# Four moves in a Perceiver block's hand-ordered loop: an earlier query load, an earlier self-attention context, split latent-sum copies, later setup steps

## The reference

```python
def attend(x, latents, mask, ...):            # x = ctx_1024, latents = layernorm(x)
    xn = layernorm(x, ln_x_g, ln_x_b)
    ln = layernorm(latents, ln_l_g, ln_l_b)
    q = ln @ Wq                                # 16 heads of 64
    kv = concatenate((xn, ln), axis=1) @ Wkv
    sim = einsum('bhid,bhjd->bhij', q, k)      # masked keys: -max
    out = einsum('bhij,bhjd->bhid', softmax(sim), v)
    return layernorm(out @ Wout, ln_o_g, ln_o_b)
x = x + attend(ctx_1024, _layernorm(x), mask, ...)
x = x + self_attention(_layernorm(x), Wq, ..., slopes)   # 64 rows, 16 heads of 8, ALiBi
x = x + feed_forward(_layernorm(x), ...)       # fake-quantised, scale from max|x| of all rows
```

## Time and profile before

| | |
|---|---|
| median of 3 runs | 866.89 us (865.94 to 867.53) |
| the profiled execution | 870.95 us |
| its span | 869.2 us |
| granted clock over the span | 0.956 |
| body 0, body 1 | 45.1, 54.3 us |
| a body of the loop (13 of them) | 47.07 us |
| PE, DVE, ACT, POOL busy in such a body | 45.6, 33.5, 34.6, 31.8 us |

### The profile page before, as it was taken

How to read it: one execution, slowest core, us unless ns; L and a number is a source line. 1 busy time by engine, 2 the same in 40 slices (tenths; PEclk the granted TensorE clock), 3 DMA queues, 4 the chain that set the end, 5 groups by cost and what they waited for, 6 DMA issues and landing times.

```text
span 869.2 us, 22523 instructions
## 1 busy us (share of the span) xinstructions
PE 780.4 (90%) x7063; PEld 423.7 (49%) x7063; DVE 605.6 (70%) x1515; ACT 587.0 (68%) x1017; POOL 521.7 (60%) x660
## 2 busy tenths in 40 slices
PE   5697899999999999999999999999999999997753
PEld 4343444545455455545454545545554545454412
DVE  5787566676777776666767677767666776756487
ACT  5387577776767676868777676767676877763242
POOL 3277356676757666666767675766666676764101
PEclk9799899999999999999999999999999999999655
DMA  6212212121221112121212122110212121200001
GB/s 191 56 42 81 71 43 68 43 62 52 57 56 52 49 26 63 41 72 38 71 41 61 52 57 56 54 48 26 62 41 72 39 71 40 67 17 16 4 0 49
DMA packets 98349, 45.86 MB, mean 53 GB/s; under 512 B 65956, under 2 KB 90376, under 8 KB 98184
## 3 DMA queue, kind: packets, MB, share of 16 engines
q1 hardware_dynamic: 98256, 45.37, 18.8%
q10 hardware_dynamic: 56, 0.05, 0.0%
HBM read 25.70 MB, written 3.27 MB: 33 GB/s over the span
## 4 chain that ended last, share of the span: by engine, by line
PE 65%; DVE 19%; ACT 7%; issue 7%; POOL 1%; DVEq 1%; DMA 1%; ACTq 1%; SPq 0%; POOLq 0%
PE bank L1399 14%; PE bank L1458 7%; DVE mx L1799 7%; PE bank L1362 7%; PE bank L1317 5%; PE bank L1366 5%; PE bank L1364 4%; PE bank L1475 3%; PE bank L1519 3%; PE bank L1334 3%; PE bank L1504 2%; PE bank L1494 2%; ACT arena L1080 2%; ACT arena L1065 2%; DVE xtT_l L1782 1%
## 5 line engine op out<-in xcount | busy, mean ns | idle before, releaser
L832 POOL TENSOR_TENSOR p<-arena,p 128x512 f16<-128x512 f32 x256 | 299.5, 1170 | 180.3 <-ACT arena L1065 179.5
L1062 ACT ACTIVATE p<-bank,maskbias 128x512 f16<-128x512 f32 x224 | 155.2, 693 | 138.2 <-PE bank L1366 137.6
L1799 DVE TENSOR_REDUCE mx<-bank 128x1 f32<-128x512 f32 x256 | 165.8, 685 | 37.9 <-PE bank L1334 36.6
L1399 PE MATMUL bank<-p,xv 128*128 128x512 f16 (+1 forms) x768 | 183.9, 382 | 5.2 <-ACT arena L1080 2.7
L1065 ACT ACTIVATE arena<-bank,maskbias 128x512 f32<-128x512 f32 x224 | 154.3, 689 | 0.0
L1399 PEld LDWEIGHTS bank<-p,xv 128*128 128x128 f16 (+1 forms) x768 | 58.0, 97 | 73.2 <-issue 23.1
L1795 DVE TENSOR_TENSOR qkl_l<-bank,qkl_h 128x512 f16<-128x512 f32 x64 | 41.1, 686 | 71.1 <-ACT qkl_h L1048 71.1
L1362 PE MATMUL bank<-qkc_h,xtT_h 128*128 128x512 f16 (+1 forms) x256 | 87.1, 390 | 0.0
L1334 PE MATMUL bank<-xtT_h,qkc_h 128*128 128x448 f16 x256 | 86.5, 359 | 0.0
L1366 PE MATMUL bank<-qkc_h,xtT_l 128*128 128x512 f16 (+1 forms) x256 | 85.4, 381 | 0.0
L1364 PE MATMUL bank<-qkc_l,xtT_h 128*128 128x512 f16 (+1 forms) x256 | 85.2, 380 | 0.0
(11 more groups left out here) (266 smaller groups left out, 1532.3 us busy)
## 6 DMA issues: line engine op xcount, KB each, us to landing
arena<-den_dram SPq DMA_DIRECT2D x62, 128.0 KB, 3.2
qkc_h<-arena SPq DMA_DIRECT2D x30, 256.0 KB, 2.4
qkc_l<-arena SPq DMA_DIRECT2D x30, 256.0 KB, 2.4
raw<-in_ctx SPq DMA_DIRECT2D x32, 192.0 KB, 2.5
raw<-in_ctx SPq DMA_DIRECT2D x64, 32.0 KB, 2.2
lt<-lt_dram SPq DMA_DIRECT2D x60, 32.0 KB, 2.1
arena<-in_L_xattn_Wkv SPq DMA_DIRECT2D x1, 1024.0 KB, 7.1
ltT_dram<-x_all SPq DMA_DIRECT2D x4, 256.0 KB, 2.9
```

The source lines that it names most:

```text
L832: g.tensor_tensor(p_halves[0:r, slot, 1, :], p_all[0:r, (plan.halves_made(0, k, t) - 1) % 2, :], p_halves[0:r, slot, 0, :], ALU.subtract). ...
L1062: a.activation(p_halves[0:r, slot, 0, :], sbank[t % SRING][0:r, :], ACT.Exp, bias=bias)
L1399: op = mm(bk[:, :], halves_of[at, row, :], p_halves[at, slot, prob, :], start=tile < 2 and n == 0, stop=last and n == 2)
L1799: v.tensor_reduce(mx[:, hq_tile, part:part + 1], bk[:, 0:width], AX.X, ALU.max).then_inc(s_jobs_taken, 1)
```

## The change

1. The load of `lq` (SP L603, `load_queries`) stood at the head of body i; it now stands in the second half of the body before, behind the context load. It is issued there in the last body of the loop too for a pair that doesn't exist, so `ltT_dram` is longer by two batches, filled by one more store.
2. The self-attention context (CX) gets a function of its own, called ahead of the step's jobs: on DVE it now stands behind MAX 0 instead of behind MAX 2.
3. RDEN of the odd batch stands at t = 7 instead of 5; `final` (XF) is called behind `tail`.
4. ACT's 32-bit exponential (part 1 of `probs`) is issued after the latents' sum copies at t = 2.
5. Late setup: the tables give blocks 1 to 3 other steps, a new table `ROOT_AT` gives POOL's root, the ALiBi table moves from step 18 to 16, and the stores of the blocks move among SP's loads.

```diff
-LATE = dict(wv=[0, 1, 2, 4], lt=[None, 6, 10, 17], aw=[7])
-BLOCK_AT = {1: (1, 4, 7), 2: (7, 8, 11), 3: (9, 14, 17)}
-HALVES_AT = {1: (6, 7), 2: (9, 10), 3: (15, 16)}
-ALIBI_AT = 18
+LATE = dict(wv=[0, 1, 2, 4], lt=[None, 9, 17, 25], aw=[7])
+BLOCK_AT = {1: (-1, 8, 11), 2: (1, 15, 18), 3: (9, 24, 27)}
+ROOT_AT = {1: 1, 2: 3, 3: 11}
+HALVES_AT = {1: (9, 11), 2: (17, 19), 3: (25, 27)}
+ALIBI_AT = 16
...
-    RDEN=(3, 5), MOVE=11, ST1=[3, 4, 5, 6], YN=[6, 7], XB=8, ST2=8, M0=9, P0=9, X1=10, X1B=17, M1=10, P1=11,
+    RDEN=(3, 7), MOVE=11, ST1=[3, 4, 5, 6], YN=[6, 7], XB=8, ST2=8, M0=9, P0=9, X1=10, X1B=17, M1=10, P1=11,
...
-                        if k == 0 and since and not last:
-                            load_queries(plan, i + 1)
                         if since and k == 0:
                             move_queries(plan, i, 1)
                             rden_spread(b - 2, par)
...
                             load_ctx(plan, b + 2, par)
+                        if k == 1 and not last:
+                            load_queries(plan, i + 2)
...
+                        if k == 1 and since < 2:
+                            for j in ((1,), (3,))[since] if plan is WINDOW else ((1, 2, 3), ())[since]:
+                                store_block(j)
...
-                        probs(plan, i, k, t)
+                        probs(plan, i, k, t, 0)
+                        for h in range(2):
+                            if t == LAG + min(h, plan.LAT - 1):
+                                copy_latents_part(plan, b, i, k, h)
+                        probs(plan, i, k, t, 1)
                         background(plan, i, since, s, self_exp)
                         prep(plan, i, last, s)
...
-                        for h in range(2):
-                            if t == LAG + min(h, plan.LAT - 1):
-                                copy_latents_part(plan, b, i, k, h)
...
+                    if (kind, k) == ("lt", 3) and since:
+                        pe.wait_ge(s_yn_done, 2)
...
                 body(0, 0, False)
                 body(1, 1, False)
+                pe.wait_ge(*late_done("lt", 3))
...
                         prep(plan, i, last, s - 0.5)
+                        background(plan, i, since, s, self_context)
                         prep(plan, i, last, s)
...
                         background(plan, i, since, s, tail)
+                        background(plan, i, since, s, final)
```

More of the change, by code:

```diff
@@ L348, in program @@
         s_ctx_loaded = [es.enter_context(nc.semaphore(f"ctx_loaded{k}")) for k in range(2)]
-        ltT_dram = nc.dram_tensor("ltT_dram", [2, D, TOK], F16).ap()
+        ltT_dram = nc.dram_tensor("ltT_dram", [2, D, TOK + 2 * M], F16).ap()
         lt_dram = nc.dram_tensor("lt_dram", [TOK, 2 * D], F16).ap()
@@ L665, in store_transposed @@
                 sp.dma_start(ltT_dram[:, :, 512 * j:512 * j + 512].rearrange("s d q -> d s q"), ltT_all[:, j, :, :]).then_inc(s_lat_stored, 16)
+                if j == 3:
+                    sp.dma_start(ltT_dram[:, :, TOK:TOK + 2 * M].rearrange("s d q -> d s q"), ltT_all[:, j, :, 512 - 2 * M:512]).then_inc(s_lat_stored, 16)
             x_pairs = x.rearrange("(a b) q d -> (b q) a d", b=2)
@@ L739, in body @@
                             rden_rows(b - 1, 1 - par, pair)
-                        if not since and k == 1:
-                            store_block(1)
+                        if since == 1 and k == 0 and plan is WINDOW:
                             store_block(2)
-                        if since == 1 and k == 0:
-                            store_block(3)
                         if k == 0:
@@ L749, in attention @@
                 body(1, 1, False)
-                sp.wait_ge(s_lat_stored, 128)
+                sp.wait_ge(s_lat_stored, 144)
                 with sp.Fori(2, PAIRS - 1) as i:
@@ L814, in late_weights @@
             def late_weights(s):
-                for j, (moments, _, _) in BLOCK_AT.items():
-                    if s == moments + 1:
+                for j in BLOCK_AT:
+                    if s == ROOT_AT[j]:
                         latents_rstd(j)
@@ L1048, in prep, with probs @@
                             a.activation(heads_of(qkl_h, job.index, odd), by_batch(both[odd]), ACT.Copy).then_inc(s_qk_hi, 1)
-            def probs(plan, i, k, t):
+            def probs(plan, i, k, t, part):
                 b = i * 2 + k
                 gg, tile, r, slot = b * plan.STEPS + t, plan.steps[t][0], plan.rows(t), slot_of(plan, k, t)
+                bias = zrow[0:r, :] if tile == 0 else maskbias[0:r, k, plan.chunk(tile):plan.chunk(tile) + 1]
+                if part == 1:
+                    if (k, t) in plan.SPLIT:
+                        made = plan.halves_made(i, k, t)
+                        if happened(made - 2):
+                            act.wait_ge(s_p_lo, made - 2)
+                        a.activation(p_all[0:r, (plan.halves_made(0, k, t) - 1) % 2, :], sbank[t % SRING][0:r, :], ACT.Exp, bias=bias).then_inc(s_probs_ready, 1)
+                    return
                 act.wait_ge(s_scores_ready, gg + 1)
@@ L1058, in probs @@
                     act.wait_ge(s_maskbias_ready, b + 1)
-                bias = zrow[0:r, :] if tile == 0 else maskbias[0:r, k, plan.chunk(tile):plan.chunk(tile) + 1]
                 if (k, t) in plan.SPLIT:
-                    made = plan.halves_made(i, k, t)
                     a.activation(p_halves[0:r, slot, 0, :], sbank[t % SRING][0:r, :], ACT.Exp, bias=bias)
-                    if happened(made - 2):
-                        act.wait_ge(s_p_lo, made - 2)
-                    a.activation(p_all[0:r, (plan.halves_made(0, k, t) - 1) % 2, :], sbank[t % SRING][0:r, :], ACT.Exp, bias=bias).then_inc(s_probs_ready, 1)
                 else:
@@ L1233, in setup, with late_weights @@
                     op.then_inc(s_setup_made, 1)
-            def late_weights(s):
+            def late_weights(s, since):
                 for kind, k in late_at(s):
@@ L1446, in tail @@
                         if not happened(p):
-                            pe.wait_ge(*late_done("lt", 3))
+                            pe.wait_ge(*late_done("lt", 2))
                         if happened(p) and not plan.own:
@@ L1551, in body @@
                         if since < 2:
-                            late_weights(s + 2 * plan.STEPS * since)
+                            late_weights(s + 2 * plan.STEPS * since, since)
                         if last and k == 1:
@@ L1828, in centred, with self_context, drained @@
                 return v.tensor_scalar(dst, src, smv[:, r, 0:1], srs[:, r:r + 1], ALU.subtract, ALU.mult)
+            def self_context(plan, p, s):
+                at, two = plan.at, tail_banks(plan)[1]
+                if s == at["CX"]:
+                    dve.wait_ge(s_attn_b, p * 7 + 5)
+                    src = two[:, 0:8 * 18].rearrange("p (a b e) -> p a b e", b=2, e=AE + 1)
+                    v.reciprocal(sden[:, :, :].unsqueeze(3), src[:, :, :, AE:AE + 1]).then_inc(s_sden_ready, 1)
+                    dve.wait_ge(s_sden_ready, p + 1)
+                    v.tensor_tensor(cx[:, :].rearrange("p (a b e) -> p a b e", b=2, e=AE), src[:, :, :, 0:AE],
+                                    sden[:, :, :].unsqueeze(3).to_broadcast([P, 8, 2, AE]), ALU.mult).then_inc(s_cx_ready, 1)
+            def drained(plan, p, s):
+                self_context(plan, p, s)
+                tail(plan, p, s)
+                final(plan, p, s)
             def tail(plan, p, s):
@@ L1893, in tail @@
                     v.tensor_reduce(smax[:, :], tsc[:, :, :], AX.X, ALU.max).then_inc(s_smax_ready, 1)
[L1894 to L1900, removed]
                 if s == at["X2"]:
@@ L1906, in tail, with final @@
                     moments(x2[:, :], 2).then_inc(s_moments_b, 1)
-                if s == at["XF"]:
+            def final(plan, p, s):
+                if s == plan.at["XF"]:
                     v.tensor_copy(x2_all[:, bass.ds(p, 1), :].rearrange("p o d -> p (o d)"), x2[:, :])
@@ L1930, in body @@
                         more = not (last and k == 1)
+                        if not since and s == 0:
+                            late_weights(-1)
                         prep(plan, i, last, s - 0.5)
+                        background(plan, i, since, s, self_context)
                         prep(plan, i, last, s)
@@ L1947, in attention @@
                 body(PAIRS - 1, 2, True)
-                drain_pairs(plan, tail, 0, 15)
+                drain_pairs(plan, drained, 0, 15)
             dve.wait_ge(s_early_ready, 1)
@@ L1956, in _ @@
                 attention(WHOLE)
-            drain_pairs(None, tail, 15, DRAIN_STEPS)
+            drain_pairs(None, drained, 15, DRAIN_STEPS)
             dve.wait_ge(s_pair_done, PAIRS)
```

## The result

The changed kernel takes 880.75 us (median of 4 runs, 880.68 to 881.46) where the kernel before takes 867.21 (865.94 to 868.9, 4 runs): the ratio is 1.0157, with a 95% interval of 1.0138 to 1.0175. It is 13.5 us slower; forecast were 851.9 us and a range of 846.5 to 861. The profiled execution has a span of 879.0 us.

A forecast was written before the change was run, and what follows sets the result against it. PE's own work was taken to bound the loop, all but 1.5 us of a 47.06 us body. Loop 5.5 plus setup 9.5 gave 15.0 us, so 866.89 - 15.0 = 851.9 us; range 846.5 to 861.

The forecast's parts named there:

- RDEN later: value 0: End of a loop body on DVE: RDEN's 0.41 us fits in xtT_l's 0.51 idle for ACT, so value 0.
- rival 1: Loop body's end: copy held by POOL's L832, KEXP ahead of XF, QP 1 1.4 us later; 870.1 us, chance 0.17.
- CX ahead of MAX 1: Loop, DVE: CX fits in idle time before the MAX pair; 0.13 us a body, bounds 0 and 0.40.
- The wait at MAX 5: Loop, PE waiting for DVE: the idle 0.31 goes, and most of it comes back at MT, grown by 0.2.
- Sum copies: Loop, step 2 on ACT: copies 0.5 us earlier end the values' wait; 0.27 us a body, bounds 0.1 and 0.27.
- Early `lq`: Loop, QP 0: load issued some 28 us ahead; the wait only moves to QP 1; value 0, upper bound 0.21.
- Loop bodies without the collision: Loop bodies of 46.67 us instead of 47.06, with XF behind the copy and before KEXP.
- The setup: Bodies 0 and 1: moved setup work shortens PE's waits and low-clock stretches; 9.5 us gained, bounds 6 and 12.
- the waits of 3.82, 1.40 and 1.63: Body 1: start gains 4.2 us, maxima 2.4 plus 1.2 for a low-clock stretch; about 0.5 and 0.6 of waiting left.
- the waits for DVE of 0.91, 0.77 and 1.31: Body 0: these waits, 2.99 us, shrink as block 1's centring leaves the chain ahead of MT; 1.8 of 3.5 gained.
- POOL did become the bound: Body 0: POOL's subtractions, root and low half crowd into the last third; half of the 1.31 wait stays.

The follow-up runs named there:

- e9: The changed kernel with RDEN of the odd batch moved between the copy to x2_all and XF, still at the body's end: 856.78 us.
- e2: The kernel before with only RDEN of the odd batch moved to t = 7: 899.32 us.
- e1: The changed kernel with only RDEN of the odd batch put back at t = 5: 853.24 us.
- e3: The changed kernel with x2_all written by a second addition out of PSUM ahead of X2, instead of by the copy: 857.87 us.
- e10: The changed kernel with RDEN of the odd batch at t = 6, ahead of X2: 859.99 us.
- e5: The changed kernel with RDEN at t = 5 and CX put back behind MAX 2: 857.89 us.
- e6: The changed kernel with RDEN at t = 5 and the sum copies put back behind the 32-bit exponential: 858.22 us.
- e7: The changed kernel with RDEN at t = 5 and CX, sum copies and lq load all put back, leaving only the setup moves: 860.79 us.
- e11: The changed kernel with RDEN at t = 5, ACT's xtT_h between step 0's exponentials, and POOL waiting for XF at the end of loop bodies: 853.04 us.

## Why the prediction was wrong

**The step that failed is the term "RDEN later: value 0".** It was priced by length: 0.41 us against a cover of 0.51 ahead of `xtT_l`. The length did fit; e9 shows it, with RDEN as late and a body of 46.67. What it did was to change which of two engines came first at a place where only one goes at a time. That mechanism stood in the text as rival 1, with its place and condition, and was given 0.17; it is what happened, each time that XF of a pair ended a body of the loop. The outcome lies outside the range because I left rival 1 out of it.

**Where rival 1 was decided, and why I took the wrong side.** The first half was right within 0.01: the copy was to start 0.19 us behind L832 and started 0.20 behind (467.70 and 467.50). The second half hung on XF being 0.05 us ahead of KEXP. KEXP was on time: 1.11 us behind the start of the subtraction by the forecast (419.94 and 418.83), 1.12 in the run (468.62 and 467.50). XF was late: 1.07 by the forecast, 1.16 in the run (468.66), so 0.04 behind KEXP. The error is in how I took the copy's end. I read XF's row as a release 0.91 behind the start of the subtraction and set the copy's own 0.23 on top. The rows show something simpler: the entry of a held instruction ends 1.23 to 1.25 us behind that start, be it the copy (0.23 alone) in the changed kernel and e2 or XF (0.34 alone) in the kernel before, e1, e3, e9 and e10. The row at 419.13 had this number (420.19 less 418.96 is 1.23). With it the copy's entry ends at 420.06 in the forecast's terms and XF's begins 0.08 before that, at 419.98, behind KEXP's 419.94: in hindsight the rows at hand pointed, narrowly, to the slow case. Besides, the one contest that I had seen, at 416.13, went to POOL. What the chip itself compares when both engines are ready isn't shown; only the order of the entries and the outcome agree in every body.

**Its price was too small in two terms.** I gave 1.4 us a body, for 13 bodies, of which 12 have the wait; QP 1 starts 5.53 us into a body instead of 3.83, so 1.7. The missing 0.3 is the end of DVE's loop, which used to lie under the wait for ACT: the last row of DVE's timeline above shows 0.32 of issue between `amax` and `xtT_l`. And I did not count that a wait of 2.5 us can lower the clock, though the earlier trace rows showed this in body 1. Bodies 2 to 14 of the changed kernel take 634.3 us, those of e1 607.4: 26.9 more. Of this 12 x 1.72 = 20.6 are the wait (body 2 has no XF of a pair before it to hold), and the other 6.3 the four bodies with a stretch of low clock. Rival 1 with both would have read 851.9 + 20.6 + 6.3 = 878.8. The 2.0 us left lie ahead of the loop: bodies 0 and 1 together are 2.1 us longer than in e1: 0.9 in body 1, where RDEN late costs too, and 1.2 in body 0, which varies between runs as said above.

**Right, with their measured sizes.** CX ahead of MAX 1: forecast 0.13, measured 0.12 (e5). The wait at MAX 5 is back in e5, as the forecast said, but its remainder didn't go to MT, which was to wait 0.2 longer: MT waits 0.29 with and without the move. It went to the job ahead of it, the transpose of `xh`, which starts 0.86 us behind the values in e1 and 0.64 in e5. Sum copies: 0.27 and 0.27 (e6). Early `lq`: 0 and 0 (e7 less e5 and e6); the wait moved from QP 0 to QP 1, 0.26 + 0.32 becoming 0.75 (the entries hide a little of each). The load is issued about 20 us ahead of QP 0 (447.80 for a body that begins at 466.55), not 28. Loop bodies without the collision: 46.67 and 46.66. The whole without it: 851.9 and 853.24; with a spread of 3 us between groups, the 1.3 says little.

**The setup.** Forecast -9.5 for bodies 0 and 1 (90.0 us); measured 91.6 in the changed kernel and 89.56 in e1, 89.60 in e7. Body 1 has a clock of 1.00; of the waits of 3.82, 1.40 and 1.63 1.47 and 0.59 are left, with a new one of 0.26 at QC, and no stretch like the earlier trace rows. RDEN late costs here too: the 1.47 is 0.52 in e1. In body 0 the waits for DVE of 0.91, 0.77 and 1.31 became two of 0.46 and 0.68, and POOL did become the bound behind them, with waits of 0.88 and 0.60 for its low halves.

**The Trainium skill's rule,** "SBUF — State Buffer", § SBUF: two separate sides, that of a DVE instruction which needs the port pair shared with GpSimd and a GpSimd one, whoever starts first has the pair for the whole instruction, fits three rows: copy 1.04 behind POOL's subtraction (0.23 alone), XF 1.94 behind KEXP, and XF 0.35 in e11, where POOL was made to wait. That section doesn't say who goes first when both stand ready; here POOL got in between DVE's back-to-back instructions.

## What to carry to other kernels

Before you move a short instruction on DVE into a gap, list the operations of DVE and POOL that work between tiles in SBUF around the new place, in order of start, and ask whether any pair changes its order: a change of order can cost up to the length of the other engine's instruction, however short the one that you moved. A cover of 0.1 us is no cover. Where a rival hangs on such a margin, look for what is constant over many rows (here when a held entry ends), and if none is found give it an even chance and let the range reach it. A wait that comes back each iteration may also cost clock; price it with and without. And a move that delays a store also delays every load behind it in the same queue, as in e2.

## What the runs showed of the hardware

- An instruction's duration in the profile includes its being held: the same copy of 128x128 shows 0.23 and 1.04 us, the same XF 0.35, 1.06 and 1.94. Held behind POOL's subtraction of 128x512 (1.16 us), either ends 1.23 to 1.25 us behind its start.
- With an operation of each engine ready when POOL's subtraction ended, the DVE instruction that had been waiting went first, and then POOL's ahead of the next of DVE, with 0.04 us between the two entries (468.62 and 468.66).
- An idle time of PE of 2.5 us was followed by a stretch at 1.2 GHz in four of twelve bodies of the changed kernel, and by none in the eight others with a wait of the same length; what tells them apart stayed open. The drop costs 1.4 to 1.8 us each time.
